# Half of a rotary step moved from the vector engine to ScalarE and GpSimd, in an attention and spiking feed-forward kernel

## The reference

```
h = layernorm(x) * (1 + ca) + sa
q, k, v = split(h @ qkv_w.T + qkv_b)         # 16 heads of 8
q, k = rope(q), rope(k)                      # [x1*cos - x2*sin, x1*sin + x2*cos]
attn = softmax(where(causal, q k^T / sqrt(8), -1e9))
x = x + ga * ((attn v) @ proj_w.T + proj_b)
h = layernorm(x) * (1 + cb) + sb
y = square(relu(h @ W_fc.T)) @ W_proj.T
x = x + gb * (number of spikes of y in 5 steps) / 5
```

## Time and profile before

| | |
|---|---|
| median of 3 runs | 489.86 us (484.31 to 490.41) |
| profiled execution: its time / its span | 488.89 us / 487.2 us |
| mean granted TensorE clock | 0.916 of 2.4 GHz |
| busy: PE / DVE / ACT / POOL | 425.2 / 317.8 / 256.0 / 123.7 us |

### The profile page before, as it was taken

One profiled execution on the slowest core, in us unless ns is written; L12 is line 12 of the kernel. 1 busy time (PEld: TensorE's weight loads), 2 busy tenths in 40 slices (PEclk: granted clock), 3 DMA queues, 4 the chain that ended last, 5 costly groups with the idle time before them and its releaser, 6 DMA issues.

```text
span 487.2 us, 14412 instructions
## 1 busy us (share of the span) xinstructions
PE 425.2 (87%) x6007; PEld 253.6 (52%) x6007; DVE 317.8 (65%) x719; ACT 256.0 (53%) x445; POOL 123.7 (25%) x159
## 2 busy tenths in 40 slices
PE   3448999889999999999999999999999999988752
PEld 2214564455546565565556654656556656645422
DVE  2768776747873978478865687388837674720735
ACT  1111465456476555755685447656665476666220
POOL 7624020501342141404240323213240310130210
PEclk9865699669999989999999699999999899999958
DMA  6166514141313232233214241323133220010000
GB/s 198 51 170 191 149 40 112 57 122 49 106 51 102 69 108 63 70 100 111 71 56 121 60 101 53 103 63 105 50 96 78 74 81 5 26 30 20 23 0 22
DMA packets 26043, 38.45 MB, mean 79 GB/s; under 512 B 5794, under 2 KB 20714, under 8 KB 23690
## 3 DMA queue, kind: packets, MB, share of 16 engines
q1 hardware_dynamic: 25978, 37.53, 26.8%
HBM read 26.35 MB, written 8.65 MB: 72 GB/s over the span
## 4 chain that ended last, share of the span: by engine, by line
PE 67%; DVE 16%; issue 4%; POOL 4%; ACT 4%; DMA 4%; SPq 1%; POOLq 0%; ACTq 0%; DVEq 0%
PE s_bank L447 15%; PE o_bank L498 12%; PE t_bank L480 10%; PE d_bank L554 6%; PE d_bank L547 5%; DVE negmax L778 4%; PE a_bank L518 4%; PE s_bank L453 3%; PE t_bank L485 2%; DMA den<-o_raw 2%; PE a_bank L525 2%; PE a_bank L467 2%; PE d_bank L537 2%; DVE xn L794 2%; DVE rot_s L814 2%
## 5 line engine op out<-in xcount | busy, mean ns | idle before, releaser
L778 DVE TENSOR_REDUCE negmax<-s_bank 128x1 f32<-128x448 f32 (+7 forms) x368 | 194.3, 566 | 99.9 <-PE s_bank L453 98.5
L664 ACT ACTIVATE probs<-t_bank 128x512 f32<-128x512 f32 x288 | 167.0, 596 | 118.0 <-PE t_bank L485 114.4
L447 PE MATMUL s_bank<-kf,qf 72*64 72x448 bf16 (+7 forms) x1024 | 127.1, 315 | 10.8 <-DVE negmax L778 10.5
L480 PE MATMUL t_bank<-qf,kf 74*64 74x512 bf16 (+7 forms) x1024 | 115.6, 297 | 4.2 <-ACT probs L664 4.1
L447 PEld LDWEIGHTS s_bank<-kf,qf 72*64 72x64 bf16 x1024 | 49.6, 114 | 101.8 <-DVE negmax L778 62.4
L498 PE MATMUL o_bank<-probs,v 128*32 128x512 f32 (+7 forms) x1024 | 92.5, 436 | 0.0
L453 PE MATMUL s_bank<-causal,identb 128*64 128x64 bf16 x1024 | 74.9, 202 | 0.0
L485 PE MATMUL t_bank<-causal_t,identb 128*64 128x64 bf16 x1024 | 65.2, 197 | 0.0
L480 PEld LDWEIGHTS t_bank<-qf,kf 74*64 74x64 bf16 x1024 | 41.4, 114 | 27.7 <-ACT probs L664 10.3
L485 PEld LDWEIGHTS t_bank<-causal_t,identb 128*64 128x64 bf16 x1024 | 49.1, 114 | 10.8
L453 PEld LDWEIGHTS s_bank<-causal,identb 128*64 128x64 bf16 x1024 | 49.4, 117 | 0.2
(11 more groups left out here) (106 smaller groups left out, 386.7 us busy)
## 6 DMA issues: line engine op xcount, KB each, us to landing
qf<-q_scr SPq DMA_DIRECT2D x15, 576.0 KB
kf<-k_scr SPq DMA_DIRECT2D x45, 192.0 KB
q_scr<-parts SPq DMA_DIRECT2D x24, 128.0 KB, 1.7
k_scr<-parts SPq DMA_DIRECT2D x24, 128.0 KB, 1.7
xa<-in_x SPq DMA_DIRECT2D x8, 256.0 KB, 3.5
o_t<-o_raw SPq DMA_DIRECT2D x60, 32.0 KB, 2.0
rden<-r_scr SPq DMA_DIRECT2D x15, 128.0 KB
out_y<-count SPq DMA_DIRECT2D x7, 256.0 KB, 2.3
```

Of the source, the lines that this page charges most:

```text
L447: nc.tensor.matmul(bank[C * a:C * (a + 1), col:col + keys], qf[0:FR, slot, 2 * p + a, C * i:C * (i + 1)], kf[0:FR, slot, 2 * p + a, 0:keys ...
L480: nc.tensor.matmul(bank[C * a:C * (a + 1), col:col + w], kf[0:KX, slot, 2 * p + a, C * kb:C * (kb + 1)], qf[0:KX, slot, 2 * p + a, C * kb: ...
L664: nc.scalar.activation(probs[:, v, :], t_bank[u % 2][:, :], ACT.Exp, scale=SCALE).then_inc(e_done, 1)
L778: last = nc.vector.tensor_reduce(own[:, i, p:p + len(same)], cols, AX.X, ALU.max, negate=True)
```

## The change

From batch 1 on, ScalarE copies the bank with the bias added, from each 64 partitions to the partner's (`swap_halves`, two instructions, line of their own), into `rot_s[:, 0]`. GpSimd multiplies this copy by the sines (`sines`, one instruction of 128 partitions) into `rot_s[:, 1]`, and adds as before. The vector engine makes the cosine product alone (`cosines`), waits for both copies before it (so that its semaphore can free the bank), and does it in slots 26 and 30. The casts stand one slot later. The sine table is rolled by 64 partitions on the host to fit. Batch 0 is made as before.

```diff
+            def swap_halves(b, qk):
+                act.wait_ge(a_ready, 4 * b + QK + qk + 1)
+                reach(act, sines_done, 2 * (b - 1) + qk)
+                act.wait_ge(whole_done, 1)
+                for to, of in ((slice(0, 64), slice(64, P)), (slice(64, P), slice(0, 64))):
+                    nc.scalar.activation(rot_s[to, 0, :], a_bank[of, :], ACT.Identity, bias=bqk_sb[of, qk:qk + 1],
+                                         scale=1.0).then_inc(swapped, 1)
...
+            swap_halves(1, 0)
             for j in range(2):
                 take_part(1, 0, j)
+            swap_halves(1, 1)
...
-            TAKE_AT = {-8: (0, 0), -6: (0, 1), -4: (1, 0), -2: (1, 1)}
+            SWAP_AT = {-11: 0, -7: 1}
+            TAKE_AT = {-7: (0, 0), -5: (0, 1), -3: (1, 0), -1: (1, 1)}
...
+                if at - PER_BATCH in SWAP_AT and b + 2 < NB:
+                    swap_halves(b + 2, SWAP_AT[at - PER_BATCH])
...
+            def cosines(b, qk):
+                dve.wait_ge(a_ready, 4 * b + QK + qk + 1)
+                reach(dve, whole_done, 2 * (b - 1) + qk + 1)
+
+                dve.wait_ge(swapped, 2 * (2 * (b - 1) + qk + 1))
+                nc.vector.scalar_tensor_tensor(rot_c[:, qk, :], a_bank[:, :], bqk_sb[:, qk:qk + 1], cos_sb[:, :],
+                                               ALU.add, ALU.mult).then_inc(a_free, 1)
...
-            for step in range(3):
-                rotary(1, 0, step)
+            cosines(1, 0)
             for k in range(7):
                 maxima(k)
-            for step in range(3):
-                rotary(1, 1, step)
+            cosines(1, 1)
...
-            ROTARY_AT = {-11: (0, 0), -10: (0, 1), -9: (0, 2), -7: (1, 0), -6: (1, 1), -5: (1, 2)}
+            COSINES_AT = {-10: 0, -6: 1}
...
+            def sines(b, qk):
+
+                pool.wait_ge(swapped, 2 * (2 * (b - 1) + qk + 1))
+                pool.wait_ge(whole_done, 2 * b + qk)
+                nc.gpsimd.tensor_tensor(rot_s[:, 1, :], rot_s[:, 0, :], sin_sb[:, :], ALU.mult)\
+                    .then_inc(sines_done, 1)
...
             for qk in range(2):
+                sines(1, qk)
                 rotary_sum(1, qk)
...
+                    sines(b + 2, 0)
                     rotary_sum(b + 2, 0)
                     left(b + 2, 0, 1)
                     left(b + 2, 0, 2)
+                    sines(b + 2, 1)
                     rotary_sum(b + 2, 1)
```

More of the change, by code:

```diff
@@ L245, in adaln_kernel @@
         rotated = sem("rotated")
+        swapped = sem("swapped")
+        sines_done = sem("sines_done")
         whole_done = sem("whole_done")
@@ L813, in rotary @@
                                       (slice(64, P), slice(0, 64), rot_s, sin_sb))[step]
-                nc.vector.scalar_tensor_tensor(dst[to, qk, :], bank[of, :], bqk_sb[of, qk:qk + 1], table[of, :],
+                nc.vector.scalar_tensor_tensor(dst[to, qk, :], bank[of, :], bqk_sb[of, qk:qk + 1], table[to, :],
                                                ALU.add, ALU.mult).then_inc(rotated if step < 2 else a_free, 1)
@@ L945, in _ @@
                         normalise1(b + 2)
-                    if at - PER_BATCH in ROTARY_AT:
-                        rotary(b + 2, *ROTARY_AT[at - PER_BATCH])
+                    if at - PER_BATCH in COSINES_AT:
+                        cosines(b + 2, COSINES_AT[at - PER_BATCH])
                 if at == NU + 7:
@@ L1041, in deviation2 @@
                 inverse_deviation(b, mv2, ve2, rs2, var2_done, eps2_done, rs2_done)
+            def sines(b, qk):
[3 more added lines that the diff above has]
+                    .then_inc(sines_done, 1)
             def rotary_sum(b, qk):
                 pool.wait_ge(a_free, 3 * b + QK + qk + 1)
-                nc.gpsimd.tensor_tensor(whole[:, qk, :], rot_c[:, qk, :], rot_s[:, qk, :], ALU.add)\
-                    .then_inc(whole_done, 1)
+                reach(pool, sines_done, 2 * (b - 1) + qk + 1)
+                nc.gpsimd.tensor_tensor(whole[:, qk, :], rot_c[:, qk, :], rot_s[:, qk if b == 0 else 1, :],
+                                        ALU.add).then_inc(whole_done, 1)
             def left(b, qk, j):
@@ L1113, in _ @@
             deviation1(1)
+            pool.wait_ge(rotary_loaded, 16 * 2)
             for qk in range(2):
+                sines(1, qk)
                 rotary_sum(1, qk)
@@ L1193 @@
         "cosn": c(np.cos(angles).astype(np.float32)),
-        "sinn": c((np.sin(angles) * signs).astype(np.float32)),
+        "sinn": c(np.roll((np.sin(angles) * signs).astype(np.float32), 64, 0)),
         "place": c(np.stack([source, source_sum], 1)),
```

## The result

The changed kernel takes 531.57 us (median of 4 runs, 530.19 to 533.88) against 490.13 us: 1.089 times as long, 95% interval 1.083 to 1.095. The profiled execution took 533.88 us with a span of 532.1 us.

The account below looks back on a forecast made before the run. ScalarE's then GpSimd's queue before slot 32's transposes was taken to bound PE: 5 x (2.85 + 1.3) = 20.8, batch 0 +1.0, clock +5.0, start-up 0, on 488.9 gives 515.7, said as 515 us; range 502 to 527.

Parts of the forecast that it names:

- What bounds the kernel: Slots 24 to 32: ScalarE's queue, then GpSimd's, ends last; PE idles 0.91 us before the transposes in batches 1 to 5.
- part 1: Vector engine loses 21.0 us of products; PE gains 0 in batches 1 to 5, a 1.21 us wait goes in batch 0.
- Batch 0: PE at half clock, no squares; the transposes of slot 32 come 1.0 us late, the mrow wait stays hidden.
- "faster" rival: Vector engine sets PE's pace; its waits and the half clock from 88 to 105 go: 471 or 480 us; chance 0.05.
- Part 2: ScalarE's queue from slot 29: copy pair 1.2 us plus moved slot start the cast of q's rest 1.58 us later.
- Part 3: GpSimd's queue before slot 32: k's sine product adds 1.27 us; with ScalarE's delay the transposes begin 2.85 us later.
- Part 4: SP's queue: mrow DMA issued 3.6 us after the transposes' start T, so PE waits 1.3 us at the next slot 0.
- Part 5: Longer stalls likely halve TensorE's clock in slots 33 to 35; cost taken as 1.0 us for each of five batches.
- heavy-clock rival: Each longer stall brings 17 us of half clock like that after 88: 5.5 us per batch, 537 us; chance 0.10.
- only the product counts: Rival: ScalarE's queue has slack, the transposes of slot 32 move by GpSimd's 1.27 us only: 496.5 us; chance 0.10.
- the maxima are held back behind cosines: Rival: cosines waits for ScalarE's copies, so PE waits on line 447; at most some tenths each; chance 0.03 (the rest).

Follow-up runs that it names:

- the filled kernel: Changed kernel with three more fp32 matmuls on TensorE before the transposes of slot 32 in batches 1 to 5: 512.05 us, 1.052 times the kernel before.
- the mended kernels: Changed kernel and kernel before, both with maxima split first, q's casts at 28 and 30, k's at 33 and 35, mrow DMA issued earlier: 498.74 and 496.41 us.
- the repaired changed kernel: Changed kernel with maxima split before k's sine product, q's casts at 28 and 30, k's at 33 and 35, mrow DMA issued earlier: 498.74 us.

## Why the prediction was right in kind and wrong in size

**What bounds the kernel, and part 1.** Right. The relief of 21 us was 22.4 and gave back 3 us of PE's waits. Batch 0 was forecast 1.0 us late and its transposes came at 95.74, as before (95.73): the clock was full from 88 to 94, where it had been at half. The "faster" rival had that in it, the forecast had not.

**Part 2.** The cast of q's rest was forecast 4.75 us after the bank and came after 5.0. The copies were priced at 1.2 us a pair and took 1.42 from the start to the next instruction (median 682 ns each); the seven instructions behind them took 3.48 us, forecast 3.5. By the formula of the Trainium skill, page "ScalarE: Activation LUTs", section "What ACT_TABLE_LOAD costs", one takes 0.71 us, an estimate, and overlaps with its neighbour by about 93 ns; the length nearly agrees, but these copies did not overlap, neither with each other nor with the exponential behind them.

**Part 3.** The product takes 1.26 us and its semaphore 0.15 more. In sum the wait grew by 4.08 - 0.91 = 3.17 us, forecast 2.85. The forecast was low by 0.3 a batch, 1.6 us in five.

**Part 4.** The order was right: the `mrow` DMA is issued at T + 3.9 (forecast T + 3.6), and at full clock, in the filled kernel, PE waits 1.12 to 1.17 for it (forecast 1.3). In the changed kernel it never shows, since PE at half clock comes to slot 0 late (at T + 8.0 in batch 2). The 6.5 us of the sum were not there as a wait.

**Part 5 is the step that failed**, a term of the sum mis-sized. It had the clock fall behind these waits, and that was shown by the filled kernel; but its price was too small. The forecast put 1.0 us a batch here beyond the 1.3 of the `mrow` wait, which part 4 adds and part 5 takes off again because half clock covers it: 2.3 us a batch for the clock in all. PE's matmuls took 27.5 us longer, 5.5 a batch. Two choices made it small. The length: of stretches of 3.4, 7 and 10 us (0, 1.4 and 2.7 us beyond the 1.3) I took a price under that of the middle one, though those behind the waits are 9.2 us on average (46 in five batches), and the rest of the 54 us more of half clock lies elsewhere, where nothing was priced. The loss: 0.4 us per us, where (452.7 - 425.2) / (88.7 - 34.7) gives 0.51. By these figures the five stretches cost 46 x 0.51 = 23.5 us, an estimate, where the forecast had 5 x 2.3 = 11.5. The heavy-clock rival had 6.8 a batch and 537 us, with the stretch after 88 us as its pattern; the measured 531.57 lies nearer to it than to 515. I gave it 0.10 because one row stood for it, but there was no row for a wait of 4 us that did otherwise. With the measured terms: 3.17 x 5 + 4.4 in batch 0 = 20.3 before line 469, + 27.5, - 3 elsewhere = 44.8, which is the 44.9 that the span grew.

**The rivals.** That only the product counts (496.5) fell with the filled kernel and with the late casts in the kernel before, whose wait grew by 1.08 with no product at all; and without the product the changed kernel still takes 506.97 us at the least. That it is faster, the vector engine being the bound, fell too: where both kernels have their queues mended it gains nothing that can be measured. That the maxima are held back behind cosines does not show: 9.2 us for line 449, 10.5 before.

**What stays open.** Which wait brings the clock down, and for how long, was not settled: it fell behind every wait of 4.08 us, behind some of 2 and 1.5, and at times behind 0.76, and what followed was 3 to 12 us of half clock behind 4.08 and 3 to 24 behind 0.76. And why the mended kernels do not beat the kernel before: their waits in the slots of the change are gone and others have grown.

## What to carry to other kernels

Before work is moved off an engine, look whether PE's waits in the slots of that work name this engine; if they name the queue that receives the work, the move lengthens the path by the work and by everything that was reordered for it. An instruction that others wait for (here the split of the maxima) belongs ahead of bulk work on a queue that is worked in order. Price a new idle gap of TensorE at the gap plus what the clock takes afterwards, and take that from the long stretches at half clock that the trace already has, not from the short ones; here the second was larger than the first.

## What the runs showed that was not expected

- Behind a wait of 4.08 us PE stayed at half clock for 10 to 12 us in four batches of five, and for 3 us in one, though it was busy without a pause; 54 us more at half clock cost 27.5 us. Filling 2.84 of those 4.08 us with useless matmuls made the changed kernel 20 us faster.
- Two copies between the halves of the partitions on ScalarE, 64 x 512 fp32 with a bias from a tile, ran strictly one behind the other at 0.71 us apart, while its exponentials, squares and casts of 128 x 512 just behind them, 0.6 us each, follow each other after 0.5.
- The same kernel spreads by 22 to 26 us from run to run on the chips of the experiments (481.10 to 507.28 for the kernel before). One profile of each kernel was kept, so that the clock makes this spread is likely and not shown: the repaired changed kernel had a mean granted clock of 0.926 in its run of 485.02 us and of 0.875 in that of 521.30, but its run of 496.56 had 0.928.
